# A two-layer graph kernel on one core: moments on GpSimd, later row stores and one low half in four on GpSimd

## The reference

```python
h = relu(layernorm(x))                      # eps 1e-5
Wh = h @ W
src, dst = Wh @ a[:F], Wh @ a[F:]
e = leaky_relu(src + dst.T, 0.2)
att = softmax(where(adj > 0, e, -9e15), axis=1)
h_prime = att @ Wh
gi = h_prime @ w_ih.T + b_ih                # a GRU cell: gates r, z, n
gh = h @ w_hh.T + b_hh
x = x + (1 - z) * n + z * h
h = relu(layernorm(x))
out = x + adj @ (h @ W1.T + b1)
```

## Time and profile before

| | |
|---|---|
| Median of 3 runs | 1555.94 us (1554.92 to 1555.95) |
| Profiled execution, its own time | 1554.47 us |
| Its span in the trace | 1552.9 us |
| TensorE (PE) busy | 1485.6 us, 96% of the span |
| VectorE (DVE) busy | 1386.0 us, 89% |
| ScalarE (ACT) busy | 1369.6 us, 88% |
| GpSimd (POOL) busy | 136.2 us, 9% |
| Mean granted TensorE clock | 0.984 of full speed |

### The profile page before, as it was taken

One profiled execution on the slowest core, in us unless ns is written; L12 is line 12 of the kernel. 1 busy time (PEld: TensorE's weight loads), 2 busy tenths in 40 slices (PEclk: granted clock), 3 DMA queues, 4 the chain that ended last, 5 costly groups with the idle time before them and its releaser, 6 DMA issues.

```text
span 1552.9 us, 35381 instructions
## 1 busy us (share of the span) xinstructions
PE 1485.6 (96%) x13262; PEld 1304.4 (84%) x13262; DVE 1386.0 (89%) x2256; ACT 1369.6 (88%) x1972; POOL 136.2 (9%) x98
## 2 busy tenths in 40 slices
PE   5477999999999999999999999999999999999998
PEld 5356888888888888888888888888888888888887
DVE  8997999999999999999999999997579877766684
ACT  5779999999999999999999999996185998777785
POOL 5000011001100010001000100010000000000000
PEclk9778999999999999999999999999999999999999
DMA  8858999999999999999999999996386999888860
GB/s 314 298 204 332 365 350 360 352 366 353 355 357 370 352 349 353 374 351 357 359 365 345 362 362 355 349 360 265 122 354 238 408 361 352 308 304 310 321 228 16
DMA packets 96380, 502.93 MB, mean 324 GB/s; under 512 B 9599, under 2 KB 38985, under 8 KB 75337
## 3 DMA queue, kind: packets, MB, share of 16 engines
q1 hardware_dynamic: 78328, 444.54, 76.1%
q10 hardware_dynamic: 18000, 57.74, 9.8%
HBM read 418.32 MB, written 83.92 MB: 323 GB/s over the span
## 4 chain that ended last, share of the span: by engine, by line
PE 92%; DVE 5%; ACT 1%; issue 1%; DMA 0%; POOL 0%; DVEq 0%; ACTq 0%
PE ACC L1014 57%; PE ACC L1104 29%; PE GP L1040 2%; PE GP L1043 2%; PE GQ L1061 1%; ACT M L506 1%; DVE M L659 1%; DVE JK L642 1%; DVE TB L733 1%; DVE AE L728 1%; DVE JK L728 1%; PE TG L1027 0%; PE TG L1050 0%; DVE JK L646 0%; DVE M L751 0%
## 5 line engine op out<-in xcount | busy, mean ns | idle before, releaser
L1014 PE MATMUL ACC<-TB,M 128*128 128x258 f16 x8192 | 927.2, 275 | 41.8 <-DVE M L751 30.7
L1014 PEld LDWEIGHTS ACC<-TB,M 128*128 128x128 fp8e4 x8192 | 804.5, 98 | 150.7 <-issue 43.2
L506 ACT ACTIVATE M<-SB,dsteep 128x256 fp8e4<-128x256 f32 x1273 | 526.2, 538 | 0.0
L516 ACT ACTIVATE JK<-X 128x3328 uint8<-128x3328 uint32 x124 | 373.2, 3010 | 0.0
L692 DVE TENSOR_SCALAR Y<-X 128x4096 fp8e4<-128x4096 f32 x128 | 291.9, 2280 | 5.9 <-DMA X<-in_adjb_dram 5.5
L605 ACT ACTIVATE TB<-TB 128x8192 uint8<-128x8192 fp8e4 x32 | 225.0, 7030 | 76.5 <-DVE TB L890 71.7
L1104 PE MATMUL ACC<-WG,X 128*128 128x256 f16 x2048 | 225.5, 273 | 0.0
L1104 PE MATMUL ACC<-WG,TB 128*128 128x256 f16 x2048 | 225.4, 273 | 0.0
L1104 PEld LDWEIGHTS ACC<-WG,X 128*128 128x128 fp8e4 x2048 | 200.4, 98 | 23.2
L1104 PEld LDWEIGHTS ACC<-WG,TB 128*128 128x128 fp8e4 x2048 | 200.4, 98 | 23.1
L743 DVE TENSOR_SCALAR M<-SB,nd 128x256 fp8e4<-128x256 f32 x775 | 213.7, 345 | 0.0
(11 more groups left out here) (145 smaller groups left out, 786.9 us busy)
## 6 DMA issues: line engine op xcount, KB each, us to landing
X<-in_adjb_dram SPq DMA_DIRECT2D x128, 2048.0 KB, 9.8
mask_bytes<-Y SPq DMA_DIRECT2D x128, 512.0 KB, 5.1
M<-in_adjb_dram ACTq DMA_DIRECT2D x24, 1920.0 KB, 9.8
X<-mask_bytes SPq DMA_DIRECT2D x16, 2048.0 KB, 9.5
TB<-mask_bytes SPq DMA_DIRECT2D x16, 2048.0 KB, 9.1
M<-in_adjb_dram ACTq DMA_DIRECT2D x4, 2048.0 KB, 11.9
M<-in_xb_dram SPq DMA_DIRECT2D x8, 512.0 KB, 8.3
h_rows<-M SPq DMA_DIRECT2D x8, 512.0 KB, 3.9
```

The costliest lines, as they stand in the source:

```text
L506: ins = nc.scalar.activation(rows(mask1(c), jj), SB[u][:, :], ACT.Sigmoid, scale=STEEP, bias=dsteep[:, j:j + 1], saturate=False)
L516: nc.scalar.activation(junk[:, 0:SEEN], X[c % 2][:, 0:SEEN].bitcast(u32), ACT.Sign, accum_out=nz[:, bass.ds(k, 1), at:at + 1].rearrange("p ...
L1014: ins = nc.tensor.matmul(A[t][m][:, 0:2 * TW], rows((mask1, mask2)[m](c), jj)[:, t * P:(t + 1) * P], TB[:, c * JC + jj, m, 0:2 * TW], star ...
```

## The change

In the first stage only groups 0 and 1 are still combined on DVE. For groups 2 to 7 DVE only takes the statistics, two groups at a time and further ahead, and GpSimd combines the even and odd halves of the statistics itself, for 16 blocks at once (`pair_moments`: seven small operations and the power). The split of the GRU weights on GpSimd waits until DVE has normalised everything (`p_hd`, 16). The row stores move: that of q = 0 behind k = 9, of 1 behind k = 11, of 2 behind k = 13, those of 3 to 7 behind k = 15; the two adjacency loads stay at k = 7 and k = 15, the latter behind the five row stores.

The scale of 2048 moves into the bias of the exponentials (+ log 2048), so L720 goes, and product i = 0 no longer waits for the second exponential. In row block 0 the low half of i = 3, 7, 11 and 15 is made by GpSimd (`t_lp`). TensorE, the count of block 1 and the next product into the same buffer wait for it. `d_hi`, `d_hh` and `k_w` share semaphores with what changed, so their counts are adjusted.

```diff
+        px = [JK[:, 740 + 20 * i:740 + 20 * i + 16] for i in range(2)]
...
-                    if k % 2:
-                        q = k // 2
+                    if k == 7:
+                        sp.dma_start(X[0][:, :], adjb[0, :, :]).then_inc(c_in[0], 16)
+                    for q in range(*((k - 9) // 2, (k - 7) // 2) if 9 <= k < 15 and k % 2 else (3, 8 if k == 15 else 3)):
                         sp.dma_start(h_d[:, q * 8:(q + 1) * 8, :], H[:, q * 8:(q + 1) * 8, :]).then_inc(p_hout, 16)
-                    if k in (7, 15):
-                        b = k // 15
-                        sp.dma_start(X[b][:, :], adjb[b, :, :]).then_inc(c_in[b], 16)
+                    if k == 15:
+                        sp.dma_start(X[1][:, :], adjb[1, :, :]).then_inc(c_in[1], 16)
...
-                for q in range(4):
+                def pair_moments(p):
+                    at = slice(p * 16, p * 16 + 16)
+                    mean_e, part_e, mean_o, part_o = [stx[:, at, i:i + 1].rearrange("p t k -> p (t k)") for i in (1, 2, 4, 5)]
+                    mean = mvx[:, at, 0:1].rearrange("p t k -> p (t k)")
+                    pool.wait_ge(p_st, 2 * p + 2)
+                    nc.gpsimd.tensor_tensor(px[0], mean_e, mean_o, ALU.add).then_inc(p_ag, 1)
+                    nc.gpsimd.tensor_tensor(px[1], part_e, part_o, ALU.add).then_inc(p_ag, 1)
+                    pool.wait_ge(p_ag, p * 6 - 5)
+                    nc.gpsimd.tensor_scalar(mean, px[0], 0.5, None, ALU.mult).then_inc(p_ag, 1)
...
+                    nc.gpsimd.tensor_tensor(sdx[:, at], px[1], px[0], ALU.add).then_inc(p_sd, 1)
+                    pool.wait_ge(p_sd, p + 2)
+                    nc.gpsimd.tensor_tensor(rsx[:, at], sdx[:, at], half[:, 0:1].to_broadcast([P, 16]), ALU.pow).then_inc(
+                        p_rs, 2)
+
+                for q in range(2):
                     deviation(q)
+                pair_moments(1)
...
-                for q in range(4, 8):
-                    deviation(q)
+                for p in range(2, 4):
+                    pair_moments(p)
+                pool.wait_ge(p_hd, 16)
                 pool.wait_ge(wt_in, 64)
...
+                for i in range(3, 16, 4):
+                    pool.wait_ge(t_hi, i + 1)
+                    j, m = i // 2 * 8, i % 2
+                    nc.gpsimd.tensor_tensor(TB[:, j:j + 8, m, TW:2 * TW], PB[i % 2], TB[:, j:j + 8, m, 0:TW],
+                                            ALU.subtract).then_inc(t_lp, 1)
                 each_row_block(pool, slot)
...
                 stats(0)
+                stats(1)
                 for q in range(8):
-                    if q < 7:
-                        stats(q + 1)
                     normalised(q)
+                    if q in (0, 1, 3):
+                        for ahead in range(q + q % 2 + 2, q + q % 2 + 4):
+                            halves_stats(ahead)
                     if q == 0:
                         dve.wait_ge(p_wa, 1)
                         nc.vector.tensor_copy(wext[:, 0:2], GP[:, 0:2]).then_inc(p_ab, 1)
...
-                        for n, table in enumerate((bt, dt_)):
-                            dve.wait_ge(p_exp, n + 1)
-                            nc.vector.tensor_scalar(table, table, TSCALE, None, ALU.mult).then_inc(t_sc, 1)
...
                                     table_product(i)
                                     table_product(i + 1)
                                     table_low(i)
-                                    table_low(i + 1)
+                                    if i % 4 == 0:
+                                        table_low(i + 1)
...
-                            pe.wait_ge(t_lo, 4 * (c + 1))
+                            pe.wait_ge(t_lo, 3 * (c + 1))
+                            pe.wait_ge(t_lp, c + 1)
```

More of the change, by code:

```diff
@@ L1 @@
 from contextlib import ExitStack
+import math
 import concourse.bass as bass
@@ L206, in binary_adjacency @@
         d_hh, d_hl = sem("d_hh"), sem("d_hl")
+        t_lp = sem("t_lp")
+        p_ag = d_hh
         g_sum = p_wa
@@ L396, in deviation @@
                         p_rs, 1)
-                for q in range(4):
+                def pair_moments(p):
[7 more added lines that the diff above has]
+                    nc.gpsimd.tensor_scalar(mean, px[0], 0.5, None, ALU.mult).then_inc(p_ag, 1)
+                    pool.wait_ge(p_ag, p * 6 - 4)
+                    nc.gpsimd.tensor_scalar(px[1], px[1], 1.0 / F, EPS, ALU.mult, ALU.add).then_inc(p_ag, 1)
+                    pool.wait_ge(p_ag, p * 6 - 3)
+                    nc.gpsimd.tensor_tensor(px[0], mean_e, mean, ALU.subtract).then_inc(p_ag, 1)
+                    pool.wait_ge(p_ag, p * 6 - 1)
+                    nc.gpsimd.tensor_tensor(px[0], px[0], px[0], ALU.mult).then_inc(p_ag, 1)
+                    pool.wait_ge(p_ag, p * 6)
+                    nc.gpsimd.tensor_tensor(sdx[:, at], px[1], px[0], ALU.add).then_inc(p_sd, 1)
[3 more added lines that the diff above has]
+                for q in range(2):
                     deviation(q)
+                pair_moments(1)
                 pool.wait_ge(p_wa, 1)
@@ L512, in count @@
                     if isinstance(g, int) and g == 1 and c == 0:
-                        act.wait_ge(t_lo, 16)
+                        act.wait_ge(t_lo, 12)
+                        act.wait_ge(t_lp, 4)
                     wait(act, c_cnt, (g - 1) * CS + c)
@@ L638, in _, with halves_stats @@
             def _(dve):
-                def stats(q):
+                def halves_stats(q):
                     dve.wait_ge(p_x[q], 16)
@@ L643, in stats @@
                     ins.then_inc(p_st, 1)
+                def stats(q):
+                    halves_stats(q)
                     dve.wait_ge(p_st, q + 1)
@@ L710, in _ @@
                 dve.wait_ge(p_k, 1)
-                nc.vector.tensor_scalar(kt[:, 0:1], kt[:, 2:3], -1.0, None, ALU.mult)
-                nc.vector.tensor_scalar(kt[:, 1:2], kt[:, 2:3], -SLOPE, None, ALU.mult).then_inc(p_k, 1)
+                nc.vector.tensor_scalar(kt[:, 0:1], kt[:, 2:3], -1.0, math.log(TSCALE), ALU.mult, ALU.add)
+                nc.vector.tensor_scalar(kt[:, 1:2], kt[:, 2:3], -SLOPE, math.log(TSCALE), ALU.mult, ALU.add).then_inc(p_k, 1)
                 nc.vector.tensor_scalar(sk, scol, kt[:, 2:3], 0.0, ALU.add, ALU.max).then_inc(p_sq, 1)
@@ L723, in table_product @@
                             dve.wait_ge(p_htout[b], 64)
-                        dve.wait_ge(t_sc, 2)
-                    wait(dve, t_lo, i - 1)
+                    if i < 2:
+                        dve.wait_ge(p_exp, i + 1)
+                    if i % 4 == 1:
+                        wait(dve, t_lp, i // 4)
+                    else:
+                        wait(dve, t_lo, (i - 2) // 4 * 3 + (i - 2) % 4 + 1 if i > 1 else 0)
                     j, m = i // 2 * 8, i % 2
@@ L822, in rows_step @@
                     if attending:
-                        dve.wait_ge(d_hi, 16 + qa + 1)
+                        dve.wait_ge(d_hi, 12 + qa + 1)
                         for t in range(2):
@@ L940, in judge @@
                 def judge():
[L941 removed]
+                    dve.wait_ge(k_w, 1)
                     nc.vector.tensor_reduce(bad[:, 3:4], GP[:, 0:1], AX.X, ALU.max).then_inc(k_v, 1)
```

3 lines of the change are left out of this document (1 added, 2 removed).

## The result

The changed kernel takes **1558.41 us** (median of 20 runs, 1555.43 to 1561.79), the kernel before 1555.93 (20 runs, 1553.78 to 1558.05). The ratio is 1.0016 (95% interval 1.0010 to 1.0023): 2.5 us slower, between 1.6 and 3.6. It lies within the 0.2% that I had called "no change", though its interval leaves out zero and reaches 0.23%. Forecast were +3.9 us, so the range held the time, and the size was too large by 1.4 us. Of the three outcomes the likelier one did not come: "slower by more than 0.2%" had 0.50, "within 0.2%" 0.45.

The account below looks back on a forecast made before the run. Bound by TensorE from 125.87 us and before that by a chain through DVE and ACT; stores 1.7, low half 0.6 in chunk 0 and 1.6 in chunks 1 to 3 sum to +3.9 us, 1559.8 us, range 1554.5 to 1562.3.

Parts of the forecast that it names:

- What bounds the kernel: Whole kernel: TensorE bounds from 125.87 us on; a shift of row block 0's end moves the kernel's end one to one.
- Moments on GpSimd: First stage: `wext` copy 3.1 us later, no cost on the path, ACT's last evacuation 1.2 us earlier, at about 44.0.
- C: Rival: row stores land in time, only the shared port costs; +1.1 us, 1557.0; chance 0.10.
- D: Rival: stores and port both covered, the first stage's earlier end remains; -1.1 us, 1554.8; chance 0.09.
- Row stores: End of first stage: last row store lands at 53.1 and holds ACT's first comparison; +1.7 us.
- No scaling: Dropping L720 takes 0.6 us from DVE, but cost and gain are nothing because ACT's table load holds DVE.
- The low half, chunk 0: Row block 0, chunk 0: `ones_of` waits for GpSimd's low half and ends at 62.4 instead of 61.8; +0.6 us.
- The low half, chunks 1 to 3: Row block 0: GpSimd's low half and `ones_of` run one behind the other in either order; +0.5 us per chunk, 1.6 together.
- B: Rival: GpSimd's low half does not hold DVE, only the stores cost; +1.7 us, 1557.6; chance 0.16.
- E: Rival: GpSimd's pairs grow from 5 to 8 us, or the strided low half takes 2.9; +6 us, 1561.9; chance 0.06.
- F: Rival: TensorE's clock gives back 2.0 us in the 128 matmuls after 125.87; -3.1 us on top of D; chance 0.05.

Follow-up runs that it names:

- x0_late: both_back with X[0] loaded behind k = 11 instead of k = 7 and GpSimd doing pair 2 ahead of the biases: 1558.47 us, ratio 1.0025.
- stores_only: The kernel before with the later row stores alone, moments and low halves on DVE: 1555.16 us, ratio 1.0004.
- stores_back: The change with a row store behind each odd k as before, the rest kept: 1557.37 us, ratio 1.0020.
- both_back: The change with the row stores in the old order and the copy into `wext` ahead of the extra statistics: 1557.28 us, ratio 1.0016.
- copy_first: The change with the copy into `wext` ahead of the statistics of groups 2 and 3: 1556.54 us, ratio 1.0016.
- early_no_pool: compare_early with all low halves back on DVE: 1554.02 us, ratio 0.9998.
- split_power: both_back with GpSimd's power of a pair taken in two halves of 8 instead of one of 16: 1554.48 us, ratio 1.0004.
- stage_only: The change's first stage and stores, with all low halves on DVE as in the kernel before: 1555.70 us, ratio 1.0006.
- compare_early: both_back with most of ACT's comparisons in chunks 1 to 3 of row block 0 made ahead of its high halves: 1556.25 us, ratio 1.0014.
- plain_early: The kernel before with ACT's comparisons of chunks 1 to 3 moved earlier and the log in the bias: 1552.62 us, ratio 0.9987.

## Why the prediction was right or wrong, point by point

**What bounds the kernel: right.** All shifts that belong to the change arise before 126 us, and in the twelve other kernels they reach the end of the span to within 0.4 us. The change's own profiled execution lost 1.2 us more behind that point, for reasons of its own.

**Moments on GpSimd: the copy right, the gain wrong.** The copy into `wext` was put at 14.8 and came at 14.62, X[0] at 29.1 and came at 28.73. The step "ACT's last evacuation comes at about 44.0, if nothing else is late" failed: it was 45.15, as before. I had written "Cost: none on the path by itself" of GpSimd's pairs and had read ACT's wait of 1.50 us for the landing of a column store without putting it in the sum. In the change TensorE waits 1.18 us at 29.74 for group 4, which DVE could normalise only behind GpSimd's power of pair 2 (28.43), and ACT's wait for the column store recurs with 1.44 at 38.58. Together they are more than the 1.2 us. x0_late, where the wait for the store is gone and the one for group 4 is not (1.63 at 29.14), ends at 42.9; its copy is early, too. The store alone is not the limit of the kernel before: in stores_only ACT does not wait for it, and still the reductions begin at 44.91, since there TensorE waits 1.0 us for DVE's last normalisation. The error cost nothing in the sum, since the stores covered it, but it made rivals C and D look 1.1 us better than they could be.

**Row stores: right in the trace.** X[0] took 9.1 us and not 8.4, but was issued earlier, and landed at 37.8 (forecast 37.5). The last landing was put at 53.1 and came at 52.9; ACT's first comparison followed at 52.97 (+1.58, forecast +1.7). X[1] was to land at 58.3 and landed at 58.56. stores_only shows the mechanism alone, with 0.6 us by the medians. What the step did not say is that putting the stores back gains nothing by itself (stores_back, +3.0), nor in the median of both_back (+3.2).

**No scaling: right,** no price seen.

**The low half, chunk 0: size off.** Forecast 62.4, measured 61.71. GpSimd did hold `ones_of`, which took 3.06 us instead of 2.29, but ACT's comparisons ended at 61.38, so 0.3 us are left of the 0.6. The eighteen instructions of ACT from the first comparison on took 8.41 us, not 8.74, since its two high halves among them (55.38 and 56.34) no longer waited for DVE's products, made during ACT's wait.

**The low half, chunks 1 to 3: the term that was mis-sized.** Forecast 0.5 us per chunk, measured 0.07 (60.16 to 103.89 before, 61.71 to 105.66 after, 0.22 in three chunks). I had written "70.81 + 2.2 + 2.26 = 75.3, where `combine` began at 74.78", with the loss the same in either order. It is not the same. In chunk 0 GpSimd was first and `combine` did come late. In chunks 1 to 3 DVE was first: GpSimd ended at 76.58 and `combine`, begun at 76.34, lost only the 0.1 of an overlap of 0.24. The sum of both held; but what of it reaches past the start of the next instruction is not a delay of its whole amount. The prediction had named the sign of this error, `combine` still released by ACT at the old distance, and the sign came: 14.63 to 14.67 us from one `combine` to the next, before 14.55 to 14.62. In place of 1.7 + 0.6 + 1.6 the trace has 1.25 + 0.30 + 0.22 = 1.77 at the last `combine`. From there to TensorE's 128 matmuls (125.87 before, 128.66 now) another 1.0 is added, most of it from the clock, for which no term of mine stood (0.74 in this execution; single executions of the other kernels have 0.74 to 0.89 in the same stretch, so I don't claim all of it for the change). That the total came within 1.4 us of the forecast is therefore in part luck: the terms of the sum are too large by 2.1, and what lies between 1.8 and the measured 2.5 had no term.

**The rivals.** Nearest to the result in time was B (+1.7, the port costs nothing), but not in mechanism: the port costs, it costs idle time. C and D fell with the stores; E's longer pairs did not come (4.9 to 5.4 us, not 8); F's clock went the other way in the profiled execution.

**Where the expected gain went.** DVE's 10.1 us became idle time: 4.87 us ahead of the first reduction instead of 0.93, 1.1 more in each of chunks 1 to 3 ahead of `combine`. On none of those places was DVE the engine that was waited for.

## What to carry to other kernels

Work is worth moving only where the chain of waits passes through the engine that it leaves; here a chunk's chain entered ACT before the moved instruction, and reordering ACT gained 2.0 us where the change, which relieved DVE, lost 2.5. Before a store is postponed, compare the share of the DMA at the old time and at the new one, and ask who needs the buffer behind it. And an engine that shares a port is no free second engine: when DVE became the bound, the help from GpSimd cost it 0.74 us per chunk more than doing the work itself.

## What the runs showed of the hardware that I had not expected

**The shared port is not always held for a whole instruction.** In the change GpSimd's L444 (a tensor_scalar, alone 2.13 us) began at 36.92, DVE's `ones_of` came 1.06 us later and took its undisturbed 2.29, and L444 took 4.03. copy_first shows the same (36.63 and 37.85, 2.29), and so do early_no_pool (1.23 us later) and split_power (1.09). In both_back `ones_of` came 1.36 us after the same instruction and was held to its end:

```profile
36.71 2.14 POOL L443 TENSOR_SCALAR R<-R 128x768 f32<-128x768 f32 x1 [3.44 <-DVE M L695]
38.91 2.75 POOL L445 CAST GW<-R 128x768 f16<-128x768 f32 x1
```

```profile
38.07 2.92 DVE L730 TENSOR_SCALAR Y<-X 128x4096 fp8e4<-128x4096 f32 x1 [1.45 <-DMA X<-in_adjb_dram]
```

In stage_only it came 1.33 us later and was held too (2.96 us). In the kernel before, L656 began 0.05 us into L416; the prediction says that it was let through, but it took 0.78 us where it takes 0.16 without a neighbour, so it was held for part of the time. A tensor_tensor on GpSimd did not let DVE in: `ones_of` at 58.73, 1.26 us into L464, waited for its end. The rule of the Trainium skill (SBUF — State Buffer, Who interferes with whom), one lock for the whole instruction, fits the tensor_tensors of these runs and not this tensor_scalar. In these six executions the entries up to 1.23 us were let in and those at 1.33 and 1.36 were held, but the time of entry was not varied on purpose, and why the tensor_scalar gives way in one run and not in another is open.

**What stands ahead in the queue sets a landing more than its own size.** A column store of 256 KB issued at 31.06, 2.3 us behind the 2 MB of X[0], landed after 7.44 us; one issued near 43 us, with no such load ahead of it, after 3.3, though the DMA was as busy (share 1.03 from 38 to 44 us).

**TensorE's clock in the first stage.** In both_back, split_power, compare_early, stage_only and stores_back the granted clock was 0.60 to 0.72 over four to six microseconds, part at the level of 1.2 GHz, after waits for DVE or ACT; in before, in the change and in plain_early it was 1.00 from 11 to 44 us. The wait alone does not decide it: copy_first and early_no_pool also waited up to 2.1 us for DVE and kept 1.00, early_no_pool with the same first stage as both_back. Most kernels with GpSimd's moments also scatter more: 1551.5 to 1556.3 in early_no_pool, 1551.6 to 1553.5 in plain_early; stage_only (1554.6 to 1557.0) and x0_late (1557.2 to 1559.8) do not.
